# Three regroupings in a perceiver layer, and one of four channel pairs convolved by diagonal matrices

## The chip, the cores and the metric

The kernel runs on one core of a Trainium2 chip. Its engines work side by side and meet only at semaphores: PE multiplies matrices into PSUM, DVE (VectorE), ACT (ScalarE) and POOL (GpSimd) work element by element, SP issues the transfers. The metric is the device time of one execution in microseconds; lower is better.

## What is computed

The reference is a layer of three parts with residual sums, on x of 16 x 128 x 512 and a context of 16 x 2048 x 512, all in fp32. The change touches the first and the second.

```python
x = x + xattn(layernorm(x), ctx, wq, bq, wk, bk, wv, bv, wo, bo)     # 16 heads
x = x + mamba_and_mlp(layernorm(x), ...)
x = x + ffn(layernorm(x), ...)

def _mamba(Z, ...):
    xz = jnp.einsum('bld,ed->ble', Z, in_proj_w)
    x, z = jnp.split(xz, 2, axis=-1)
    x = jax.nn.silu(_causal_dw_conv(x, conv_w, conv_b))              # 4 taps, per channel
    x_dbl = jnp.einsum('bld,ed->ble', x, x_proj_w)
    dt, Bm, Cm = jnp.split(x_dbl, [DTR, DTR + DS], axis=-1)
    dt = jax.nn.softplus(jnp.einsum('blr,dr->bld', dt, dt_proj_w) + dt_proj_b)
    # h = exp(dt * A) * h + dt * B * x;  y = sum over 16 states of h * C, step by step
    y = y + x * D
    y = y * jax.nn.silu(z)
    return jnp.einsum('bld,ed->ble', y, out_proj_w)
```

## The kernel before

It has three stages with a barrier between them: `cross_attention`, `mamba`, `feed_forward`.

**The query stretch** opens `cross_attention`. Four blocks of x (4 batches each, 1 MB) go through `normalise` on DVE (statistics, then four TENSOR_SCALARs, L339), with the reciprocal root on POOL between the two (L236, L238), sixteen transposes (L459) and 96 matmuls in two halves (L477) on PE. DVE also splits the weights in this stretch. POOL adds bo to each block after its normalisation (L242, waits for `xn_ready`), SP stores it to `x_scratch`. Two buffers in `probs` hold x, so block 2 is loaded after block 0 is stored. Then the loop over 16 batches begins, with key projections (L498) and loads of the context into `c_raw`.

**mamba** takes eight steps of two batches (256 tokens). Inner channels are eight chunks of 128, in four pairs. The recurrence runs as 32 units in a step: unit m is channel pair m // 8 and two of the 16 states. In each unit ACT fills `decay` in PSUM (a copy and four exponentials, L1073, L1077; two slots), POOL makes `drive` = dt_u * B (L939; four slots, free again when PE has summed), DVE scans (L1212) and multiplies by C (L1223), PE adds both states into `b_y` by two matmuls with the identity (L1356, semaphore `summed`). At units 8, 16, 24 and the next step's unit 0 DVE multiplies the finished pair by its gate (L1177): it waits there for PE's last b_y, and PE then starts the next pair with two matmuls for D (L1352).

Between these the next step's preparation is laid out by numbers at the top of the function, each the unit behind which a piece is issued on its engine: head projections, layernorm, transposes, x projections (units 9, 10, 11, 13), z projections (L1271; eight halves), taps on ACT and three shifted multiply-adds per chunk on DVE (L1149; units 12, 13, 14, 16), silu of u (L1008, unit 18), the x_dbl product (L1297, unit 19), dt projections (21, 23), and then softplus: ACT takes absolute value, exponential (units 25 and 27) and logarithm (L1045), POOL the rounding error of 1 + e: (e + 1) - 1 in one TENSOR_SCALAR (L906), and e minus that (L908), behind units 28 and 31; then the two sums of dt (L912, L914) and dt_u (L920). Every order is fixed in the program; an engine stops at the first wait that is not met. Steps 1 to 6 run in a loop of three turns with two steps each.

## Time and profile before

| | us |
|---|---|
| median of 3 runs | 4165.88 (4165.74 to 4169.53) |
| profiled execution | 4164.47 |
| its span, first to last instruction | 4162.3 |

| stage | us | PE busy | DVE | ACT | POOL |
|---|---|---|---|---|---|
| query stretch, 0 to 77 | 77 | 56.7 | 49.4 | 19.9 | 31.0 |
| attention, to 2424 | 2347 | 2311.5 | 1558.4 | 854.8 | 290.1 |
| mamba, first step's preparation, to 2497 | 73 | 45.9 | 23.0 | 23.7 | 6.1 |
| mamba, 256 units, to 3609 | 1112 | 944.3 | 998.1 | 691.9 | 821.0 |
| feed-forward, to 4162 | 553 | 512.5 | 244.3 | 117.7 | 57.9 |

The busy times come from the view that sums each engine over stretches of time. In a timeline a row gives start, length, engine, line, operation, output and inputs, and in brackets how long the engine stood idle before and who released it. Consecutive instructions overlap a little, so distances between starts say more than lengths. The first key projection (L498) starts at 77.15. A step of mamba takes 141.3 us: the TENSOR_SCALAR at L906 recurs at that distance, from 2610.4 to 3458.2 seven times.

### The profile page before, as it was taken

The page shows a single profiled execution, that of the slowest core. Times are in us where ns is not written, and L with a number is a line of the kernel's source. Part 1 is how long each engine was busy: PE and PEld are TensorE (multiplying, and loading weights), DVE is VectorE, ACT ScalarE, POOL GpSimd, SP SyncE. Part 2 cuts the span into 40 slices and gives each one's busy share as a digit, 9 for nine tenths or more (in the row PEclk, how much of TensorE's full clock was granted, in tenths as well). Part 3 has the DMA queues.
Part 4 walks back from the last instruction along what each step waited for, and adds up shares of the span by engine and source line. Part 5 has one row for each costly group of instructions (what it writes and reads, how often), then busy time and mean ns, then how long its engine had stood idle before and what let it go on. Part 6 is the DMA issues. An engine that isn't in the chain of part 4 may idle for free. (4 is left out here: it accounts for less than half of the span.)

```text
span 4162.3 us, 85144 instructions
## 1 busy us (share of the span) xinstructions
PE 3870.9 (93%) x34816; PEld 2798.7 (67%) x34816; DVE 2873.2 (69%) x3019; ACT 1707.9 (41%) x3434; POOL 1206.1 (29%) x563
## 2 busy tenths in 40 slices
PE   7999999999999999999999968888888887599998
PEld 6777877777787777777777755445444443288876
DVE  6667667766766776676667649889988988764433
ACT  2324423433442443344244346666566656322221
POOL 3111010111011011101100106876787678420000
PEclk9999999999999999999999989999999999899999
DMA  5010010011001001100100030211011111120000
GB/s 190 32 36 28 35 44 27 25 44 37 28 32 47 27 25 44 37 28 32 46 28 22 24 128 26 61 51 46 26 61 51 36 35 46 58 87 26 30 20 16
DMA packets 94278, 179.23 MB, mean 43 GB/s; under 512 B 7889, under 2 KB 12369, under 8 KB 93938
## 3 DMA queue, kind: packets, MB, share of 16 engines
q1 hardware_dynamic: 93938, 174.08, 12.8%
q8 instruction: 289, 4.73, 0.5%
q14 instruction: 51, 0.42, 0.0%
HBM read 148.63 MB, written 25.43 MB: 42 GB/s over the span
## 5 line engine op out<-in xcount | busy, mean ns | idle before, releaser
L230 POOL TENSOR_TENSOR c_lo<-c_raw,c_hi 128x2048 fp32r<-128x2048 f32 x64 | 294.9, 4608 | 1987.0 <-DVE c_hi L323 1987.0
L939 POOL TENSOR_TENSOR b_drive<-b_dt_u,b_bc 128x1024 f32<-128x1024 f32 x256 | 600.7, 2357 | 284.9 <-PE b_y L1356 248.7
L1356 PE MATMUL b_y<-b_drive,b_ident 128*128 128x512 f32 x1024 | 512.2, 627 | 146.7 <-DVE b_drive L1223 146.7
L412 DVE TENSOR_TENSOR prob_sums<-prob_sums,probs 128x1024 f32<-128x1024 f32 x480 | 566.7, 1222 | 114.0 <-ACT probs L295 114.0
L1212 DVE TENSOR_TENSOR_SCAN b_decay<-b_decay,b_drive 128x1024 f32<-128x1024 f32 x256 | 585.9, 2289 | 80.3 <-POOL b_drive L939 62.1
L384 DVE TENSOR_REDUCE max_parts<-scores 128x2 f32<-128x1024 f32 x512 | 601.8, 1218 | 40.3 <-PE scores L546 40.3
L295 ACT ACTIVATE probs<-scores 128x512 f32<-128x512 f32 x1024 | 529.0, 603 | 213.9 <-PE scores L577 213.9
L376 DVE SCALAR_TENSOR_TENSOR k_lo<-scores,bk_sb,k_hi 128x512 fp32r<-128x512 f32 x256 | 192.3, 751 | 562.0 <-ACT k_hi L280 561.9
L1356 PEld LDWEIGHTS b_y<-b_drive,b_ident 128*128 128x128 f32 x1024 | 188.9, 196 | 395.9 <-DVE b_drive L1223 236.4
L1077 ACT ACTIVATE b_decay<-b_dt,b_a 128x254 f32<-128x254 f32 x1024 | 425.0, 461 | 0.4
L280 ACT ACTIVATE k_hi<-scores,bk_sb 128x512 fp32r<-128x512 f32 x256 | 176.4, 689 | 603.1 <-PE scores L498 603.1
L288 ACT COPY v_sb<-scores 128x512 f32<-128x512 f32 x240 | 141.1, 588 | 668.4 <-PE scores L498 668.4
L1223 DVE TENSOR_TENSOR b_drive<-b_decay,b_bc 128x1024 f32<-128x1024 f32 x256 | 313.0, 1223 | 7.8
L577 PE MATMUL scores<-q_hi,k_lo 32*128 32x128 f32 x4096 | 305.3, 270 | 0.0
L577 PE MATMUL scores<-q_lo,k_hi 32*128 32x128 f32 x4096 | 305.1, 270 | 0.0
L577 PE MATMUL scores<-q_hi,k_hi 32*128 32x128 f32 x4096 | 291.8, 256 | 0.0
L498 PE MATMUL scores<-c_hi,wk_hi 128*128 128x512 f32 x1024 | 287.4, 402 | 0.0
L498 PE MATMUL scores<-wv_hi,c_hi 128*128 128x512 f32 x960 | 281.2, 415 | 0.0
L591 PE MATMUL o_acc<-probs,v_sb 128*32 128x128 f32 x8192 | 276.7, 276 | 1.2 <-ACT probs L295 1.2
L498 PE MATMUL scores<-c_hi,wk_lo 128*128 128x512 f32 x1024 | 274.8, 390 | 0.0
L498 PE MATMUL scores<-c_lo,wk_hi 128*128 128x512 f32 x1024 | 273.7, 389 | 0.0
L498 PE MATMUL scores<-wv_lo,c_hi 128*128 128x512 f32 x960 | 258.7, 391 | 0.0
(219 smaller groups left out, 6304.9 us busy)
## 6 DMA issues: line engine op xcount, KB each, us to landing
c_raw<-in_ctx SPq DMA_DIRECT2D x64, 1024.0 KB, 5.1
b_bc<-bc_scratch SPq DMA_DIRECT2D x128, 256.0 KB, 4.2
probs<-in_x SPq DMA_DIRECT2D x4, 1024.0 KB, 5.6
x_scratch<-probs SPq DMA_DIRECT2D x4, 1024.0 KB, 6.0
q_scratch<-v_sb SPq DMA_DIRECT2D x4, 1024.0 KB, 4.4
q_raw<-q_scratch SPq DMA_DIRECT2D x16, 256.0 KB, 2.9
attn_scratch<-attn_out_sb SPq DMA_DIRECT2D x16, 256.0 KB, 2.0
b_attn<-attn_scratch SPq DMA_DIRECT2D x8, 512.0 KB, 4.1
```

The lines of the kernel that those rows point to most:

```text
L230: pool.tensor_tensor(c_lo[:, slot], c_raw[:], c_hi[:, slot].bitcast(F32), ALU.subtract).then_inc(c_lo_ready, 1)
L295: act.activation(probs[:, (2 * t + j // 2) % 4, j % 2, :], score_bank(t, j), ACT.Exp, scale=scale).then_inc(exp_done, 1)
L384: dve.tensor_reduce(max_parts[:, g, 2 * pair:2 * pair + 2, s], max_banks[:, 2 * pair:2 * pair + 2, :], AX.X, ALU.max).then_inc(max_taken, 1)
L412: dve.tensor_tensor(part, part, probs[:, u % 4], ALU.add).then_inc(summed, 1)
L498: ins = pe.matmul(out, lhs, rhs, start=(m == 0), stop=(m == len(steps) - 1))
L577: ins = pe.matmul(banks[j][:, g * queries:(g + 1) * queries], k_part[head_rows(j), g, ts], q_part[head_rows(j), g, :], start=False, stop=last,
L591: ins = pe.matmul(o_acc[head_rows(j), g * queries:(g + 1) * queries], v_sb[:, t, h * hd:(h + 1) * hd], probs[:, (2 * t + j // 2) % 4, j % ...
L939: pool.tensor_tensor(drive[:, m % 4], dt_u[:, 2 * p:2 * p + 2, :].unsqueeze(1).to_broadcast([P, SG, 2, T]), bc[:, g, 0].unsqueeze(2).to_br ...
L1077: ins = act.activation(slot[:, q:q + group, 1:], by_batch(dt[:, par, c, :])[:, :, 1:], ACT.Exp, scale=a_neg[:, c, g * SG + s:g * SG + s + 1])
L1212: dve.tensor_tensor_scan(decay[:, m % 2], decay[:, m % 2], drive[:, m % 4].rearrange("p n c t -> p (n c t)"), 0.0, ALU.mult, ALU.add).then ...
L1223: dve.tensor_tensor(drive[:, m % 4], decay[:, m % 2].rearrange("p (n c t) -> p n c t", c=2, t=T), bc[:, g, 1].unsqueeze(2).to_broadcast([P ...
L1356: ins = pe.matmul(y_ps[:], ident[:], drive[:, m % 4, s].rearrange("p c t -> p (c t)"), start=False, stop=(g == groups - 1 and s == SG - 1) ...
```

## The change

- Query stretch: the x blocks lie in `probs`, `c_raw`, `probs`, `probs`, so three loads need no store before them. On POOL the additions of bo come later than before, each behind a following rstd or behind the first low part of the context. The first context load comes after the second x store, and the last two x stores after the last query store.
- mamba: the first half of the rounding error, (e + 1) - 1, is made by DVE behind units 25 and 27 (`round_sum`); POOL keeps the subtraction.
- mamba: silu of the gate, before at unit 30 of the step ahead (in step 0 at unit 3), is at unit 4 of its own step.
- mamba: channel pair 3 (chunks 6 and 7) is convolved on PE. POOL makes eight diagonal matrices of the taps once. ACT copies the projection to `u` (behind unit 16), PE multiplies four shifted views by the diagonals into the same PSUM bank (behind unit 15), ACT's silu reads that bank and adds the bias. Three z projection halves move one unit back (15, 16, 17 to 16, 17, 18).

```diff
@@ cross_attention
-        x_sb = [probs[:, 2 * par:2 * par + 2].rearrange("p n j d -> p (n j) d") for par in range(2)]
+        x_even, x_odd = (probs[:, 2 * n:2 * n + 2].rearrange("p n j d -> p (n j) d") for n in range(2))
+        x_sb = [x_even, c_raw[:], x_odd, x_even]
@@ sync
+            load_x(2)
+            store_x(0)
+            sp.wait_ge(x_stored, 16)
+            load_x(3)
+            store_queries(0)
+            sp.wait_ge(q_stored, 16)
+            sp.dma_start(q_raw[:], q_dram[0]).then_inc(q_loaded, 16)
+            store_x(1)
+            sp.wait_ge(x_stored, 2 * 16)
             load(0, 0)
-            for i in range(q_steps):
-                sp.wait_ge(bo_added, i + 1)
-                sp.dma_start(x_out_v[i], x_sb[i % 2]).then_inc(x_stored, 16)
-                if i + 2 < q_steps:
-                    sp.wait_ge(x_stored, (i + 1) * 16)
-                    load_x(i + 2)
+            for i in range(1, q_steps):
                 store_queries(i)
-                if i == 0:
-                    sp.wait_ge(q_stored, 16)
-                    sp.dma_start(q_raw[:], q_dram[0]).then_inc(q_loaded, 16)
+            store_x(2)
+            store_x(3)
             sp.wait_ge(q_stored, q_steps * 16)
             sp.wait_ge(x_stored, q_steps * 16)
@@ gpsimd
+            make_rstd(0)
+            make_rstd(1)
+            pool.wait_ge(bo_loaded, 16)
+            add_bo(0)
+            make_rstd(2)
+            add_bo(1)
+            make_rstd(3)
+            low_part(0, 0)
+            add_bo(2)
+            add_bo(3)
@@ mamba
-    PE_IN_Z, PE_OUT = (14, 15, 16, 17, 20, 22, 24, 25), (27, 29, 31)
+    PE_IN_Z, PE_OUT = (14, 16, 17, 18, 20, 22, 24, 25), (27, 29, 31)
...
+    DVE_M = (25, 27)
+    PE_CONV = 15
+    taken = pairs - 1
@@ gpsimd
             def rounding_error(j, h):
 
-                pool.wait_ge(exp_ready, j * 2 + h + 1)
-                pool.tensor_tensor(pool_wait_taker[:], zeros[:, 0:1], zeros[:, 0:1], ALU.add)
-                pool.tensor_scalar(e_round[h], e_neg[h], 1.0, -1.0, ALU.add, ALU.add).then_inc(rounded, 1)
                 pool.wait_ge(rounded, j * 2 + h + 1)
                 pool.tensor_tensor(e_neg[h], e_neg[h], e_round[h], ALU.subtract).then_inc(low_ready, 1)
...
+                pool.wait_ge(x_half_loaded, X_HALF_LOADED)
+                pool.tensor_tensor(tap_diag[:], ident[:].unsqueeze(1).unsqueeze(1).to_broadcast([P, 2, taps, P]),
+                                   conv_w_sb[:, 2 * taken:, :].unsqueeze(3).to_broadcast([P, 2, taps, P]),
+                                   ALU.mult).then_inc(tap_diag_ready, 1)
@@ scalar
+            def copy_last(j, par):
+                act.wait_ge(x_product, (j + 1) * pairs)
+                act.copy(u[:, par, 2 * taken:, :],
+                         work[:, x_bank(taken), :].rearrange("p (c t) -> p c t", t=T)).then_inc(x_copied, 1)
+
             def silu_u(j, par):
                 for h in range(2):
-                    act.wait_ge(x_taken, j * pairs + (h + 1) * (pairs // 2))
-                    hc = slice(h * half, (h + 1) * half)
-                    ins = act.activation(u[:, par, hc, :], u[:, par, hc, :], ACT.Silu)
+                    act.wait_ge(x_taken, j * taken + (2, taken)[h])
+                    hc = slice(h * half, min((h + 1) * half, 2 * taken))
+                    act.activation(u[:, par, hc, :], u[:, par, hc, :], ACT.Silu)
+                act.wait_ge(convolved, j + 1)
+                for cc in range(2):
+                    c = 2 * taken + cc
+                    ins = act.activation(u[:, par, c, :], work[:, x_bank(taken), cc * T:(cc + 1) * T], ACT.Silu,
+                                         bias=conv_b_sb[:, c:c + 1])
                 ins.then_inc(u_ready, 1)
@@ vector, body
+                    if m in DVE_M:
+                        round_sum(j, DVE_M.index(m))
@@ tensor
+            def convolve_last(j, par):
+                pe.wait_ge(x_copied, j + 1)
+                for cc in range(2):
+                    out = by_batch(work[:, x_bank(taken), cc * T:(cc + 1) * T])
+                    x_in = by_batch(u[:, par, 2 * taken + cc, :])
+                    for shift in range(taps):
+                        ins = pe.matmul(out[:, :, shift:], tap_diag[:, cc, taps - 1 - shift], x_in[:, :, 0:seq - shift],
+                                        start=(shift == 0), stop=(shift == taps - 1), skip_group_check=True)
+                ins.then_inc(convolved, 1)
```

On PE the place is units 14 to 16 of the first step; b_work holds projections, b_y the sum over states. Before:

```order
L1356 MATMUL b_y<-b_drive,b_ident 128x512 x2
L1271 MATMUL b_work<-b_xn_t,b_w_in 128x256 x4
L1356 MATMUL b_y<-b_drive,b_ident 128x512 x2
L1271 MATMUL b_work<-b_xn_t,b_w_in 128x256 x4
L1352 MATMUL b_y<-b_u,b_d_diag 128x256 x2
L1356 MATMUL b_y<-b_drive,b_ident 128x512 x2
```

After:

```order
L1412 MATMUL b_y<-b_drive,b_ident 128x512 x2
L1315 MATMUL b_work<-b_xn_t,b_w_in 128x256 x4
L1412 MATMUL b_y<-b_drive,b_ident 128x512 x2
L1334 MATMUL b_work<-b_u,b_tap_diag 128x256
L1334 MATMUL b_work<-b_u,b_tap_diag 128x2x127
L1334 MATMUL b_work<-b_u,b_tap_diag 128x2x126
L1334 MATMUL b_work<-b_u,b_tap_diag 128x2x125
L1334 MATMUL b_work<-b_u,b_tap_diag 128x256
L1334 MATMUL b_work<-b_u,b_tap_diag 128x2x127
L1334 MATMUL b_work<-b_u,b_tap_diag 128x2x126
L1334 MATMUL b_work<-b_u,b_tap_diag 128x2x125
L1408 MATMUL b_y<-b_u,b_d_diag 128x256 x2
```

A z projection half that stood behind unit 15 is replaced by eight matmuls with the tap diagonals.

On POOL the place is unit 28 of the first step, where x and attn are the buffers of e and of its rounded sum. Before:

```order
L939 TENSOR_TENSOR b_drive<-b_dt_u,b_bc 128x1024 x21
L905 TENSOR_TENSOR b_pool_wait_taker<-b_zeros 128x1
L906 TENSOR_SCALAR b_attn<-b_x 128x1024
L908 TENSOR_TENSOR b_x<-b_x,b_attn 128x1024
L939 TENSOR_TENSOR b_drive<-b_dt_u,b_bc 128x1024 x2
L912 TENSOR_TENSOR b_dt<-b_dt,b_attn 128x1024
```

After:

```order
L966 TENSOR_TENSOR b_drive<-b_dt_u,b_bc 128x1024 x21
L931 TENSOR_TENSOR b_x<-b_x,b_attn 128x1024
L966 TENSOR_TENSOR b_drive<-b_dt_u,b_bc 128x1024 x2
L935 TENSOR_TENSOR b_dt<-b_dt,b_attn 128x1024
L937 TENSOR_TENSOR b_dt<-b_dt,b_x 128x1024
```

Two of the three instructions between the drives are gone.

On DVE the place is units 24 and 25 of the first step. Before:

```order
L1177 TENSOR_TENSOR b_gate<-b_y,b_gate 128x512
L1223 TENSOR_TENSOR b_drive<-b_decay,b_bc 128x1024
L1212 SCALAR_TENSOR_TENSOR b_decay<-b_decay,b_drive 128x1024
L1223 TENSOR_TENSOR b_drive<-b_decay,b_bc 128x1024
L1212 SCALAR_TENSOR_TENSOR b_decay<-b_decay,b_drive 128x1024
```

After:

```order
L1219 TENSOR_TENSOR b_gate<-b_y,b_gate 128x512
L1265 TENSOR_TENSOR b_drive<-b_decay,b_bc 128x1024
L1254 SCALAR_TENSOR_TENSOR b_decay<-b_decay,b_drive 128x1024
L1265 TENSOR_TENSOR b_drive<-b_decay,b_bc 128x1024
L1196 TENSOR_SCALAR b_attn<-b_x 128x1024
L1254 SCALAR_TENSOR_TENSOR b_decay<-b_decay,b_drive 128x1024
```

The TENSOR_SCALAR stands behind the multiply of unit 25.

On POOL in the query stretch, from the first rstd on. Before:

```order
L236 TENSOR_TENSOR q_rstd<-q_moments,q_eps 128x4
L238 TENSOR_TENSOR q_rstd<-q_rstd,q_minus_half 128x4
L242 TENSOR_TENSOR probs<-probs,attn_out_sb 128x2048
L236 TENSOR_TENSOR q_rstd<-q_moments,q_eps 128x4
L238 TENSOR_TENSOR q_rstd<-q_rstd,q_minus_half 128x4
L242 TENSOR_TENSOR probs<-probs,attn_out_sb 128x2048
```

After:

```order
L244 TENSOR_TENSOR q_rstd<-q_moments,q_eps 128x4
L246 TENSOR_TENSOR q_rstd<-q_rstd,q_minus_half 128x4
L244 TENSOR_TENSOR q_rstd<-q_moments,q_eps 128x4
L246 TENSOR_TENSOR q_rstd<-q_rstd,q_minus_half 128x4
L250 TENSOR_TENSOR probs<-probs,attn_out_sb 128x2048
L244 TENSOR_TENSOR q_rstd<-q_moments,q_eps 128x4
```

The addition of bo to block 0 stood between the rstd of blocks 0 and 1 and now follows that of block 1.

## Rows read from the trace of the kernel before

**Rows 1.** Timeline of DVE: start and length in us, instruction, count, [idle before <- releaser].

```profile
2886.31 0.69 DVE L1177 TENSOR_TENSOR b_gate<-b_y,b_gate 128x512 f32<-128x512 f32 x1 [2.25 <-PE b_y L1356]
...
2888.05 2.29 DVE L1212 TENSOR_TENSOR_SCAN b_decay<-b_decay,b_drive 128x1024 f32<-128x1024 f32 x1
...
2891.51 2.29 DVE L1212 TENSOR_TENSOR_SCAN b_decay<-b_decay,b_drive 128x1024 f32<-128x1024 f32 x1
...
2903.75 2.30 DVE L1212 TENSOR_TENSOR_SCAN b_decay<-b_decay,b_drive 128x1024 f32<-128x1024 f32 x1 [1.76 <-ACT b_decay L1077]
...
2912.74 2.30 DVE L1212 TENSOR_TENSOR_SCAN b_decay<-b_decay,b_drive 128x1024 f32<-128x1024 f32 x1 [1.98 <-POOL b_drive L939]
...
2921.23 2.30 DVE L1212 TENSOR_TENSOR_SCAN b_decay<-b_decay,b_drive 128x1024 f32<-128x1024 f32 x1 [4.93 <-POOL b_drive L939]
...
2934.13 2.30 DVE L1212 TENSOR_TENSOR_SCAN b_decay<-b_decay,b_drive 128x1024 f32<-128x1024 f32 x1 [1.97 <-POOL b_drive L939]
...
2994.64 0.69 DVE L1177 TENSOR_TENSOR b_gate<-b_y,b_gate 128x512 f32<-128x512 f32 x1 [0.56 <-PE b_y L1356]
...
2996.39 2.67 DVE L1149 SCALAR_TENSOR_TENSOR b_u<-b_work,b_conv_w,b_u 128x254 f32<-128x254 f32 x6
...
3027.75 0.69 DVE L1177 TENSOR_TENSOR b_gate<-b_y,b_gate 128x512 f32<-128x512 f32 x1 [2.25 <-PE b_y L1356]
```

**Rows 2.** Timeline of POOL across units 28 to 31, same columns.

```profile
2891.05 2.36 POOL L939 TENSOR_TENSOR b_drive<-b_dt_u,b_bc 128x1024 f32<-128x1024 f32 x1 [2.34 <-PE b_y L1356]
...
2893.51 3.65 POOL L906 TENSOR_SCALAR b_attn<-b_x 128x1024 f32<-128x1024 f32 x1
...
2897.25 2.35 POOL L908 TENSOR_TENSOR b_x<-b_x,b_attn 128x1024 f32<-128x1024 f32 x1
...
2909.06 1.27 POOL L920 TENSOR_TENSOR b_dt_u<-b_dt,b_u 128x512 f32<-128x512 f32 x1
```

**Rows 3.** Timeline of DVE in the first step's preparation.

```profile
2485.04 0.69 DVE L1158 TENSOR_SCALAR b_attn<-b_x 128x1024 f32<-128x1024 f32 x1 [11.93 <-ACT b_x L1040]
```

**Rows 4.** Timeline of POOL and DVE in the query stretch.

```profile
23.60 1.02 POOL L238 TENSOR_TENSOR q_rstd<-q_rstd,q_minus_half 128x4 f32<-128x4 f32 x1
...
24.66 1.92 DVE L339 TENSOR_SCALAR prob_sums<-probs,q_moments,q_rstd 128x512 f32<-128x512 f32 x4 [1.42 <-POOL q_rstd L238]
...
56.42 1.22 DVE L323 CAST c_hi<-c_raw 128x2048 fp32r<-128x2048 f32 x1
...
56.58 5.50 POOL L242 TENSOR_TENSOR probs<-probs,attn_out_sb 128x2048 f32<-128x2048 f32 x1 [2.03 <-DVE prob_sums L339]
...
60.50 1.85 DVE L369 CAST q_hi<-q_raw 128x512 fp32r<-128x512 f32 x1
...
62.03 4.80 POOL L230 TENSOR_TENSOR c_lo<-c_raw,c_hi 128x2048 fp32r<-128x2048 f32 x1
```

**Rows 5.** Timeline of ACT from unit 28 to the next step's unit 0.

```profile
2896.87 1.28 ACT L1045 ACT_TABLE_LOAD   x1
...
2899.63 1.06 ACT L1045 ACTIVATE b_attn<-b_attn 128x1024 f32<-128x1024 f32 x1 [1.47 <-POOL b_x L908]
...
2902.05 1.66 ACT L1077 ACTIVATE b_decay<-b_dt,b_a 128x254 f32<-128x254 f32 x4
...
2907.20 1.91 ACT L1018 ACTIVATE b_gate<-b_gate 128x2048 f32<-128x2048 f32 x1
...
2916.13 0.17 ACT L1073 COPY b_decay<-b_zeros 128x8 f32<-128x8 f32 x1 [3.99 <-issue]
```

**Rows 6.** Timeline of PE: first step's x_dbl product, then units 19 to 21.

```profile
2474.21 3.64 PE L1297 MATMUL b_work<-b_u,b_w_x 128*64 128x256 f32 x16 [1.55 <-ACT b_u L1008]
...
3009.49 1.98 PE L1356 MATMUL b_y<-b_drive,b_ident 128*128 128x512 f32 x4 [1.48 <-DVE b_drive L1223]
...
3016.83 1.89 PE L1271 MATMUL b_work<-b_xn_t,b_w_in 128*128 128x256 f32 x8
...
3018.55 1.88 PE L1356 MATMUL b_y<-b_drive,b_ident 128*128 128x512 f32 x4
```

67 lines of the change are left out of this document (40 added, 27 removed).

## The prediction

> **What bounds the kernel now.** I read the busy time by stage first, then the idle times of the engine that is busiest there, then the timelines of the engines it waits for. The three stages follow one another: attention to about 2424 us, mamba to about 3620, feed-forward to the end. In mamba VectorE (DVE) is the busiest, at nine tenths in the table of stages above. One unit of its work is a scan and a multiply, 3.46 us (2888.05 to 2891.51) [rows 1], and a step has 32 of them. The bracket at a row's end is the idle time before it, and who ended it [rows 1]: per step DVE waits 2.25 us for PE's b_y at unit 24, 1.76 for ACT's decay at unit 29, 1.98, 4.93 and 1.97 for POOL's drive at units 31, 0 and 3. These five recur in all seven step boundaries to within 0.05 us (the last four add up to 10.64 us per step). POOL is late because from unit 28 on it has the rounding error (3.65 + 2.35 us, and again at unit 31) and the sums of dt to do between drives of 2.35 us each [rows 2]. So mamba is a DVE chain with holes that POOL makes; attention is bound by PE and not touched; in the stretch before it (to 77 us) PE waits for DVE.
>
> **Round sums moved from POOL to DVE.** POOL loses 3.65 us twice per step [rows 2]. DVE gains two TENSOR_SCALARs of 128x1024, behind the multiplies of units 25 and 27. The same form cost DVE 0.69 us where POOL stood idle [rows 3]. Beside a running POOL no row shows it; the nearest is the cast at 60.50: 1.85 us for 512 columns, where 2048 columns took 1.22, and it ended just after POOL's 56.58 + 5.50 = 62.08 [rows 4]. So I take it that the sum waits until the POOL instruction that is running has ended: 0.65 to 3.05 us each. The phase says how long. Count from the gate multiply at unit 24 (2886.31 = 0). POOL's drive for unit 28 started at 2891.05, released by PE's b_y of unit 24, and this release doesn't move: 4.74 to 7.10. The first sum is due at 5.2, starts at 7.1, and the next scan at 7.75 instead of 5.2: 2.55 us. POOL subtracts 7.8 to 10.15, makes two drives (the second is released by b_y of unit 26, at 13.15) until 15.5; the second sum is due at 14.75 and costs 0.75 + 0.65 = 1.4 us.
>
> What goes: ACT's logarithm needs POOL's subtraction, now at 10.15. Its fill of unit 28 starts with multiply 26 (11.3) and ends at 13.1; table load 1.28 and logarithm 1.06 [rows 5] to 15.5; table load and fill of unit 29 to 18.6, and scan 29 is due at 16.2 + 3.46 = 19.65. The 1.76 go. POOL: dt sums 16.2 to 20.9, dt_u 1.27 to 22.1, drive 31 to 24.5 (due 26.6: the 1.98 go), subtraction to 26.8, drive 0 to 29.15 (due 30.05: the 4.93 go), dt_u, drives 1 and 2 to 35.1, two dt sums to 39.8, drive 3 to 42.15, due 41.0: 1.2 of the 1.97 stay. Sum: 10.64 - 2.55 - 1.4 - 1.2 = 5.5 us per step.
>
> **Silu of the gate, from unit 30 of the step before to unit 4.** Two table loads and 1.9 us [rows 5] leave the place where ACT is pressed. At unit 4 ACT has fill 4 done at about 42.9 on the same count, silu to 46.1, table and fill 5 to 49.1; DVE comes for unit 5 at 52.1. Nothing is late there, and at the old place the wait went already: 0.
> ACT's loop has two steps per turn, and behind the branch back ACT stood 3.99 us with nothing to wait for [rows 5]. Today this is hidden under the 4.93. Then: fill 31 ends at 25.0, + 4.0, fill of unit 0 to 30.85, due 30.05. 0.8 us on two branches: 1.6 us.
>
> **The convolution of pair 3 on PE.** DVE loses six instructions at unit 16, 2.58 us from row to row (2996.39 to 2998.97, of which the first stands in [rows 1]). PE gains eight matmuls of 256 columns in fp32; four of that form take 1.72 us, from 3016.83 to 3018.55 [rows 6], so 3.45 us, with their weight loads in it. Is there room? The interval between the gate multiplies of units 16 and 24 is 33.1 us (2994.64 to 3027.75) [rows 1], and it ends with a wait for PE: from 3009.49 on [rows 6] PE works without a gap, 18.3 us. In the new order PE has from the end of b_y 15: 3.45 + 0.86 (two matmuls for D) + 3 x 1.72 (b_y 16 to 18) + 3 x 1.72 (z projections, one of them moved here) = 14.6, and then the same 18.3: 32.9 us. The old idle gaps of PE at units 17 and 19 are where it fits. b_y 15 ends some 0.2 before the multiply, so the interval becomes 32.7: **0.4 us of the 2.58** is kept, the rest turns into a longer wait for b_y at unit 24 (about 4.4 less what ACT takes, below). ACT's part is one copy for two scaled taps, and a silu in four pieces that now reads PE's result at 3.5; with it the fill of unit 19 comes 1.85 late. That lies under PE's lateness: 0. In the first step there is no cover: the z projection stands ahead of the x_dbl product, which waited 1.55 us for u [rows 6]; it comes 4.15 - 1.55 = 2.6 us later. POOL's new diagonal tiles are made while it idles: 0.
>
> **The query stretch.** The third x block no longer waits for a buffer, but little waited for it. The order on POOL matters: adding bo to block 0 now stands right behind the second rstd. Before it came after DVE's normalisation, by a wait. POOL's pow ended at 24.62 and DVE started at 24.66 [rows 4]; two POOL instructions in a row start without a gap (56.58 + 5.50 and 62.03), so POOL would be first. If the four TENSOR_SCALARs of the normalisation are held like the cast, they come 4.6 us late, and again at block 2; PE waits for them. The stretch from turn 1 to turn 2 becomes 14.2 - 0.75 + 4.6, from 2 to 3 about as long as now, less 1; the first projection of keys, at 77.15 in the table above, starts 5.1 later. The next context load waits for two x stores that are now queued behind the last query store: 0.7. Together **5.8 us lost**, bounds -1.4 and 10.
>
> **The sum.** 7 x (5.5 + 0.4) = 41.3; less 1.6, 2.6 and 5.8: 31.3 us. The profiled execution took 4164.5 (span 4162.3); it becomes 4133.2. The runs' median is 1.4 above it: **4134.5 us**.
>
> Two rules of the Trainium skill bear on this. SBUF — State Buffer, "Who interferes with whom", says that a DVE instruction in a two-port mode and a GpSimd instruction exclude each other for the whole length of the one that started first; the row at 60.50 agrees, and without the rule the two sums would cost 1.3 instead of 3.95 us and the time be 18 us lower. Runtime: NRT & Kernel Launch, "Instruction fetch mechanics", says that a taken branch to a target outside the two held blocks of instructions stalls; ACT's 3.99 us agrees, and for DVE it would give the third rival.
>
> **Rivals.** *A, the query stretch loses nothing* (DVE gets in first, or this form isn't held): 4134.5 - 5.8 = 4129. For it: 0.54 us for 512 columns is no clean double rate. Chance 0.22.
> *B, the round sums are not held:* 3.95 becomes 1.3 per step, 7 x 2.65 = 18.6 us: 4116. Chance 0.12.
> *C, DVE too stalls behind its branch back*, which is hidden today under the wait of 4.93: about 3.5 us on two turns, 4141. Against: its loop body has some 300 instructions in the order of the program, ACT's some 500. Chance 0.06.
> *D, PE is worse off than counted:* a matmul whose columns lie in two runs of 127 to 125 costs twice what the plain one of the rows does: 3.4 us per step, all at unit 24: 4158. Chance 0.09.
> *E, slower:* a held DVE instruction is not let in between two POOL instructions that follow at once. The second sum, due at 14.75, then waits through dt sums, dt_u and drive 31, to 23.8: 8.3 us per step, 58 us: 4193. It decides from a POOL queue without a gap at 15.5. Against: the cast at 60.50 got in between two such instructions, and the second took 0.2 longer. Chance 0.05.
> *F, the gain goes to a wait not seen:* 4166. Chance 0.06.
> The forecast itself: 0.40.
>
> **Numbers.** 0.2% (8.3 us) is about what a measurement tells from no change. Faster: forecast, A, B, C and half of D, 0.85 with a rest of F: 0.87. Same: half of D and most of F: 0.07. Slower: E and a rest: 0.06. The range leaves out E, F and the far half of D: 4112 (B with its slack) to 4152 (C or a cheap D).
>
> **What would show it.** Right: DVE's waits for POOL at units 31 and 0 gone, about 1 us at unit 3; TENSOR_SCALARs of 2.5 and 1.4 us on DVE; wait for b_y at unit 24 grown to 2.5 to 4.5 us; step 135.4 instead of 141.3 us; normalisations of blocks 1 and 2 with a TENSOR_SCALAR of some 5 us; first key projection at 82. Wrong: sums of 0.7 us, step of 133 or of over 139 us, a b_y wait over 6 us, first key projection before 78.

## The result, and the profile after

The changed kernel takes 4137.44 us (median of 4 runs, 4134.2 to 4138.92) against 4165.81 us before; the ratio is 0.9929, 95% interval 0.9912 to 0.9946. The prediction said 4134.5 us. The profiled execution has a span of 4136.4 us, 25.9 less than before.

Where the two executions part, from the timelines (us from the start of each):

| point | before | after | difference |
|---|---|---|---|
| first key projection | 77.15 | 82.56 | +5.4 |
| first reciprocal behind attention's last batch | 2420.34 | 2426.62 | +6.3 |
| scan of unit 0, step 0 | 2497.55 | 2506.46 | +8.9 |
| gate multiply at unit 24, step 0 | 2603.16 | 2610.89 | +7.7 |
| last gate multiply of mamba | 3604.54 | 3577.48 | -27.1 |
| end of span | 4162.3 | 4136.4 | -25.9 |

The stretches before the first scan lose 8.9 us, the eight steps win 36.0, 34.8 of them from the first step's unit 24 on; 1.2 are lost again in feed-forward. Busy times by engine, from the top of the page:

```profile
PE 3890.2 (94%) x34944; PEld 2826.2 (68%) x34944; DVE 2885.8 (70%) x2985; ACT 1706.0 (41%) x3442; POOL 1157.0 (28%) x536
```

POOL is 49.1 us less busy (1206.1 before), DVE 12.6 more: it has fourteen more sums (two had been its own in the first step's preparation), and fewer multiply-adds.

**A step's boundary.** Timeline of DVE from the gate multiply at unit 24 on, the rows that answer to [rows 1]; then POOL beside it:

```profile
2881.53 0.69 DVE L1219 TENSOR_TENSOR b_gate<-b_y,b_gate 128x512 f32<-128x512 f32 x1 [2.84 <-PE b_y L1412]
...
2885.59 1.23 DVE L1265 TENSOR_TENSOR b_drive<-b_decay,b_bc 128x1024 f32<-128x1024 f32 x1
2886.73 2.44 DVE L1196 TENSOR_SCALAR b_attn<-b_x 128x1024 f32<-128x1024 f32 x1
2889.09 2.28 DVE L1254 TENSOR_TENSOR_SCAN b_decay<-b_decay,b_drive 128x1024 f32<-128x1024 f32 x1
...
2896.02 1.64 DVE L1196 TENSOR_SCALAR b_spare<-b_mix 128x1024 f32<-128x1024 f32 x1
2897.58 2.28 DVE L1254 TENSOR_TENSOR_SCAN b_decay<-b_decay,b_drive 128x1024 f32<-128x1024 f32 x1
...
2914.17 2.30 DVE L1254 TENSOR_TENSOR_SCAN b_decay<-b_decay,b_drive 128x1024 f32<-128x1024 f32 x1 [2.66 <-POOL b_drive L966]
...
2950.73 0.69 DVE L1219 TENSOR_TENSOR b_gate<-b_y,b_gate 128x512 f32<-128x512 f32 x1 [1.67 <-PE b_y L1412]
```

```profile
2889.25 2.35 POOL L931 TENSOR_TENSOR b_x<-b_x,b_attn 128x1024 f32<-128x1024 f32 x1 [0.63 <-DVE b_attn L1196]
...
2897.07 2.80 POOL L935 TENSOR_TENSOR b_dt<-b_dt,b_attn 128x1024 f32<-128x1024 f32 x1
...
2908.23 2.35 POOL L966 TENSOR_TENSOR b_drive<-b_dt_u,b_bc 128x1024 f32<-128x1024 f32 x1
```

The waits of 1.76, 1.98 and 4.93 us at units 29, 31 and 0 are gone. In their place stand two sums of 2.44 and 1.64 us; from start to start they push the next scan back by 2.36 (2886.73 to 2889.09) and 1.56 us. At unit 0 a wait of 2.66 us stands in this step and one of 2.68 at 3189.70, the two places where the loop branches back, and in none of the others. In the other five steps the wait for POOL's drive at unit 3 is 1.25 us, against 1.97 before:

```profile
2652.97 2.30 DVE L1254 TENSOR_TENSOR_SCAN b_decay<-b_decay,b_drive 128x1024 f32<-128x1024 f32 x1 [1.25 <-POOL b_drive L966]
```

The sum of dt at 2897.07 took 2.80 us where the other sum of dt, at 2899.95, took 2.36: it started while DVE's second sum ran (2896.02 to 2897.66). So POOL is held by DVE as well.

**PE's clock.** DVE's wait for b_y at unit 8 (2950.73) is 1.67 us; it is 0 in five of the seven steps. Timeline of PE ahead of it, and the table of windows, whose fields are the window, its length, busy time and count of PE, its weight loads, DVE, ACT and POOL, then the granted clock, the DMA share and GB/s:

```profile
2938.37 1.98 PE L1412 MATMUL b_y<-b_drive,b_ident 128*128 128x512 f32 x4 [0.98 <-DVE b_drive L1265]
2943.45 2.72 PE L1412 MATMUL b_y<-b_drive,b_ident 128*128 128x512 f32 x4 [3.10 <-DVE b_drive L1265]
2946.91 3.78 PE L1412 MATMUL b_y<-b_drive,b_ident 128*128 128x512 f32 x4 [0.74 <-DVE b_drive L1265]
```

```profile
2940.00:2944.00 4.00, 0.90 (x3) 0.31 (x3) 3.96 (x3) 2.05 (x8) 3.77 (x6) 1.00 0.00 0
2944.00:2948.00 4.00, 3.26 (x6) 0.94 (x5) 3.96 (x3) 3.75 (x10) 3.92 (x4) 0.57 0.10 39
2948.00:2952.00 4.00, 4.00 (x13) 2.34 (x12) 2.33 (x3) 0.65 (x2) 4.00 (x3) 0.58 0.24 94
2952.00:2956.00 4.00, 2.60 (x8) 1.06 (x7) 3.97 (x4) 2.75 (x7) 3.29 (x2) 1.00 0.00 0
```

Four matmuls that take 1.98 us take 3.78: behind the idle 3.10 us the granted clock is 0.57 and 0.58 for two windows of 4 us, that is the lower of its two levels, 1.2 instead of 2.4 GHz, for most of them. The trace of before has such falls too. One less the granted clock, summed over windows of 2 us from 2520 to the last gate multiply, is the clock lost in the steps: 25.6 us there (15 falls of 1.7 us each) and 18.8 here (11 falls). But there DVE's six waits at units 8 and 16 add up to 3.2 us, and the six here to 6.8.

**The query stretch.** Timelines of DVE and POOL at block 1, to be read against [rows 4], and of PE at its end:

```profile
24.02 6.12 DVE L360 TENSOR_SCALAR prob_sums<-c_raw,q_moments,q_rstd 128x512 f32<-128x512 f32 x4 [1.41 <-POOL q_rstd L246]
```

```profile
22.97 1.01 POOL L246 TENSOR_TENSOR q_rstd<-q_rstd,q_minus_half 128x4 f32<-128x4 f32 x1
23.95 4.54 POOL L250 TENSOR_TENSOR probs<-probs,attn_out_sb 128x2048 f32<-128x2048 f32 x1
```

```profile
82.56 1.07 PE L519 MATMUL scores<-c_hi,wk_hi 128*128 128x512 f32 x4
```

POOL starts the addition of bo 0.07 us ahead of the four TENSOR_SCALARs, and these take 6.12 instead of 1.92 us: the addition ends at 28.49, they end at 30.14. Block 2 repeats it (42.63, 6.13 us).

### The profile page after: what moved, and what is told of

Read it like the earlier page. It is cut to its first block and busy times, and to the rows that moved or that the text cites. A ratio compares the mean times of both kernels' runs of the same rounds, so it can differ in the third digit from the quotient of the medians.

```text
span 4136.4 us, 85345 instructions
## 1 busy us (share of the span) xinstructions
PE 3890.2 (94%) x34944; PEld 2826.2 (68%) x34944; DVE 2885.8 (70%) x2985; ACT 1706.0 (41%) x3442; POOL 1157.0 (28%) x536
## 5 line engine op out<-in xcount | busy, mean ns | idle before, releaser
L1412 PE MATMUL b_y<-b_drive,b_ident 128*128 128x512 f32 x1024 | 502.9, 619 | 116.0 <-DVE b_drive L1265 116.0
```

The source lines that it names most:

```text
L1412: ins = pe.matmul(y_ps[:], ident[:], drive[:, m % 4, s].rearrange("p c t -> p (c t)"), start=False, stop=(g == groups - 1 and s == SG - 1) ...
```

## The experiments

All kernels are the changed one with the edit that is shown; the times are medians of 4 to 11 runs, the ratios are to the kernel before in the same session, which took 4164.6 to 4167.9 us.

| kernel | us | ratio to before | interval |
|---|---|---|---|
| query_old | 4131.5 | 0.9921 | 0.9907 to 0.9934 |
| sum_stt | 4151.4 | 0.9970 | 0.9958 to 0.9982 |
| conv_dve | 4132.5 | 0.9925 | 0.9911 to 0.9938 |
| sums_pool | 4172.7 | 1.0016 | 1.0007 to 1.0025 |
| gate30 | 4140.3 | 0.9946 | 0.9932 to 0.9960 |
| dve_unroll | 4132.8 | 0.9921 | 0.9907 to 0.9935 |
| sums_early | 4115.9 | 0.9883 | 0.9867 to 0.9899 |
| best1 | 4106.2 | 0.9862 | 0.9846 to 0.9877 |
| warm | 4128.8 | 0.9912 | 0.9899 to 0.9926 |
| best2 | 4097.9 | 0.9835 | 0.9821 to 0.9848 |
| best3 | 4094.6 | 0.9829 | 0.9815 to 0.9842 |
| best4 | 4092.0 | 0.9820 | 0.9807 to 0.9833 |

The four runs of the changed kernel lie between 4134.2 and 4138.9 us. Those of conv_dve (4131.3 to 4136.6) and of gate30 (4136.9 to 4145.1) overlap with them, and so do those of best2 and best3 with each other (4094.9 to 4098.5, 4092.2 to 4096.2): what is said of these small differences rests on the rows.

### The order on POOL in the query stretch (query_old)

```diff
             make_rstd(0)
-            make_rstd(1)
             pool.wait_ge(bo_loaded, 16)
             add_bo(0)
-            make_rstd(2)
+            make_rstd(1)
             add_bo(1)
+            make_rstd(2)
+            add_bo(2)
             make_rstd(3)
             low_part(0, 0)
-            add_bo(2)
             add_bo(3)
```

> The changed kernel, with bo added on POOL directly behind each block's own normalisation again (reciprocal root 0, bo 0, reciprocal root 1, bo 1, reciprocal root 2, bo 2, reciprocal root 3, first low part, bo 3); buffers, loads and stores stay as changed. The changed kernel took 4137.4 us. Theory (two TENSOR_SCALAR groups were held 4.2 us each by the addition of bo that started 0.07 us ahead of them): the groups of blocks 1 and 2 take 1.9 us instead of 6.1, the two casts of wk and wv are held 0.7 us each instead, and the first key projection comes at about 76 instead of 82.56: 6 to 7 us less, 4131. Rival (the stretch is late for another reason, such as the stores and the loads behind them on SP): first key projection at 81 or later, 4137.

Measured: 4131.5 us. Timelines of DVE, POOL and PE:

```profile
24.61 1.92 DVE L360 TENSOR_SCALAR prob_sums<-c_raw,q_moments,q_rstd 128x512 f32<-128x512 f32 x4 [1.42 <-POOL q_rstd L246]
...
30.77 1.52 DVE L337 CAST wk_hi<-v_sb 128x2048 fp32r<-128x2048 f32 x1
```

```profile
26.61 4.60 POOL L250 TENSOR_TENSOR c_raw<-c_raw,attn_out_sb 128x2048 f32<-128x2048 f32 x1 [2.03 <-DVE prob_sums L360]
```

```profile
73.95 1.07 PE L519 MATMUL scores<-c_hi,wk_hi 128*128 128x512 f32 x4
```

The group of four is back at 1.92 us, a cast pays 0.3 (and its like at 44.52 0.8), and the key projections start 8.6 us earlier than in the changed kernel (some 6.5 were expected), 3.2 earlier than before. So the new buffers and loads are worth 3.2 us, and the two moved additions cost 8.6. The medians moved by 5.9 and the spans by 8.6: the attention stretch behind, to the reciprocal of the first table, is itself 2342.2 to 2345.3 us long in the profiles of the fourteen kernels, though nothing in it differs.

### Where the gain of the boundary comes from (sums_pool, gate30)

```diff
+                pool.wait_ge(exp_ready, j * 2 + h + 1)
+                pool.tensor_tensor(pool_wait_taker[:], zeros[:, 0:1], zeros[:, 0:1], ALU.add)
+                pool.tensor_scalar(e_round[h], e_neg[h], 1.0, -1.0, ALU.add, ALU.add).then_inc(rounded, 1)
                 pool.wait_ge(rounded, j * 2 + h + 1)
...
-                    if m in DVE_M:
-                        round_sum(j, DVE_M.index(m))
```

> The changed kernel, with the round sum back on POOL (3.65 us twice per step), silu of the gate staying at unit 4. Theory (the sums are the whole gain of the step boundaries): waits for POOL of about 2.0, 4.9 and 2.0 us at units 31, 0 and 3 are back and the sums of 2.4 and 1.6 us on DVE are gone; 5.75 us more per step, less 2.7 on the two turns where DVE's wait of 2.66 at unit 0 is hidden again: 35 more, 4172. Rival (moving silu of the gate away from unit 30 has removed part of the waits): units 31 and 0 wait less than 5 us together, below 4160.

Measured: 4172.7 us. Timeline of DVE across one boundary:

```profile
2771.60 2.30 DVE L1257 TENSOR_TENSOR_SCAN b_decay<-b_decay,b_drive 128x1024 f32<-128x1024 f32 x1 [1.76 <-ACT b_decay L1118]
...
2780.57 2.30 DVE L1257 TENSOR_TENSOR_SCAN b_decay<-b_decay,b_drive 128x1024 f32<-128x1024 f32 x1 [1.95 <-POOL b_drive L969]
...
2789.06 2.30 DVE L1257 TENSOR_TENSOR_SCAN b_decay<-b_decay,b_drive 128x1024 f32<-128x1024 f32 x1 [4.93 <-POOL b_drive L969]
...
2801.96 2.30 DVE L1257 TENSOR_TENSOR_SCAN b_decay<-b_decay,b_drive 128x1024 f32<-128x1024 f32 x1 [1.97 <-POOL b_drive L969]
```

All four waits of [rows 1] are back to within 0.03 us, although silu of the gate stayed at unit 4. Without the moved sums nothing is gained at the boundary; the new place of the silu alone brings nothing. Units 24 to 0 take 37.10 us in all seven steps here, and 32.11 in the changed kernel where it does not branch.

```diff
-    ACT_Z, ACT_DBC, ACT_ABS, ACT_EXP, ACT_LOG0, ACT_GATE = (19, 20, 25, 29), 22, (24, 26), (25, 27), 28, 4
+    ACT_Z, ACT_DBC, ACT_ABS, ACT_EXP, ACT_LOG0, ACT_GATE = (19, 20, 25, 29), 22, (24, 26), (25, 27), 28, 30
...
-                        silu_gate(i, par)
+                        silu_gate(j, 1 - par)
```

> The changed kernel, with silu of the gate at unit 30 of the step before again. Theory (it has slack at either place): at unit 30 the silu and its two table loads make ACT's fill of unit 31 about 1.2 us late on DVE's scan of unit 31, but POOL's chain from unit 27 to unit 3 is not moved, so the wait of 1.25 at unit 3 becomes as much shorter: the period of a step stays 134.5 us (without lateness of PE), the time within 3 us of 4137. Rival (the place at unit 4 is part of the gain): 1.2 us or more per step is lost, 4146 or more.

Measured: 4140.3 us. Timeline of DVE:

```profile
2774.70 2.30 DVE L1256 TENSOR_TENSOR_SCAN b_decay<-b_decay,b_drive 128x1024 f32<-128x1024 f32 x1 [1.16 <-ACT b_decay L1115]
...
2789.70 2.30 DVE L1256 TENSOR_TENSOR_SCAN b_decay<-b_decay,b_drive 128x1024 f32<-128x1024 f32 x1 [0.60 <-POOL b_drive L966]
```

ACT is 1.16 us late at unit 31, and the wait at unit 3 shrinks from 1.25 to 0.60. Units 24 to 8 take 66.65 instead of 66.05 us, 0.6 us per step; the medians differ by 2.9. The move was called free at both places; it is worth a little, once the waits behind it have become short.

### What holds the sum (sum_stt, sums_early)

```diff
-                dve.tensor_scalar(e_round[h], e_neg[h], 1.0, -1.0, ALU.add, ALU.add).then_inc(rounded, 1)
+                dve.scalar_tensor_tensor(e_round[h], e_neg[h], 1.0, minus_one[:].to_broadcast([P, group * width]),
+                                         ALU.add, ALU.add).then_inc(rounded, 1)
```

> The changed kernel, with the round sum (e + 1) - 1 on DVE in the steps' units written as a SCALAR_TENSOR_TENSOR, (e + 1) + (a column of -1, broadcast), instead of a TENSOR_SCALAR. Theory (only the short form, 0.69 us for 1024 columns, is held by a running POOL instruction; a form that takes 1.2 us for 1024 columns, as the multiply does, runs beside POOL): both sums take 1.2 us instead of 2.44 and 1.64, DVE gains 1.64 us per step; POOL's chain from unit 27 to unit 3 starts 1.2 earlier and its sum of dt is no longer held 0.45, so the wait at unit 3 stays near 1.25: 1.6 to 1.7 us per step, 11.5 in seven: 4126. Rival (any DVE instruction issued at that point waits for POOL, whatever its form): 1.2 + 1.8 and 1.2 + 0.9 us: 7 us more, 4144. Second rival (the wait at unit 3 and the stall at unit 0 take it back): step time unchanged, 4137.

Measured: 4151.4 us; the theory fell. Timelines of DVE and POOL:

```profile
2617.01 2.98 DVE L1198 SCALAR_TENSOR_TENSOR b_attn<-b_x,b_minus_one 128x1024 f32<-128x1024 f32 x1
...
2625.69 1.22 DVE L1269 TENSOR_TENSOR b_drive<-b_decay,b_bc 128x1024 f32<-128x1024 f32 x1
2626.84 2.18 DVE L1198 SCALAR_TENSOR_TENSOR b_spare<-b_mix,b_minus_one 128x1024 f32<-128x1024 f32 x1
...
2902.86 1.22 DVE L1198 SCALAR_TENSOR_TENSOR b_spare<-b_mix,b_minus_one 128x1024 f32<-128x1024 f32 x1
```

```profile
2616.55 2.35 POOL L968 TENSOR_TENSOR b_drive<-b_dt_u,b_bc 128x1024 f32<-128x1024 f32 x1 [2.35 <-PE b_y L1416]
...
2625.58 2.36 POOL L968 TENSOR_TENSOR b_drive<-b_dt_u,b_bc 128x1024 f32<-128x1024 f32 x1 [0.85 <-PE b_y L1416]
2627.89 3.34 POOL L937 TENSOR_TENSOR b_dt<-b_dt,b_attn 128x1024 f32<-128x1024 f32 x1
...
2903.25 3.03 POOL L968 TENSOR_TENSOR b_drive<-b_dt_u,b_bc 128x1024 f32<-128x1024 f32 x1 [2.51 <-PE b_y L1416]
```

The long form is held as well: it ends 1.09 us after POOL's drive (2616.55 + 2.35 = 2618.90), about its own length. A multiply of the same size and pace is not: the one at 2625.69 starts 0.11 us behind POOL's drive at 2625.58 and takes its 1.22. They differ in where the inputs lie (the multiply's first is decay, in PSUM, the sum's two are in SBUF) and in the operation; no run parts the two.

The second sum shows the rest within one execution. Its length over the seven steps is 2.18, 3.32, 1.22, 2.17, 3.24, 2.82 and 2.18 us, by where POOL's drive has got to. At 2902.86 the sum starts 0.39 us ahead of the drive, takes 1.22, and it is the drive that is held: 3.03 instead of 2.35. In the four steps that differ the drive was released later, behind PE at the lower clock, in that one so late that DVE came first. From start to start the fourteen sums cost 9.4 us more than those of the changed kernel; the rival's 4144 is 7 short of the time. The rest was not followed up; PE's lost clock, summed as above, is 32.4 us in this execution against 18.8.

The Trainium skill, SBUF — State Buffer, "Who interferes with whom", states the case: a DVE instruction with both inputs in SBUF contends with a GpSimd instruction that reads SBUF. I had drawn on that section only for the two-port modes; by its other sentence the rival was the one to expect, and these rows agree.

```diff
                         end_pair(i - 1, 1 - par, pairs - 1)
+                    if not last and m in DVE_M:
+                        round_sum(j, DVE_M.index(m))
                     dve.wait_ge(scanned, i * units + m + 1)
...
-                    if m in DVE_M:
-                        round_sum(j, DVE_M.index(m))
```

> The changed kernel, with each round sum between the scan and the multiply of units 25 and 27 instead of behind the multiply, 1.14 us earlier. Nothing else is changed; the sum stays a TENSOR_SCALAR. Theory (what counts is whether a POOL instruction is under way when it is due): counted from the gate multiply of unit 24, POOL is idle until 4.74 and the sum starts at 4.03 and takes 0.7 instead of 2.44; the second is due at 11.6 and waits 0.2 for POOL to end: 0.9 instead of 1.64; DVE gains 2.4 us per step, POOL's chain starts 0.8 earlier and is not held 0.45, so the wait at unit 3 grows from 1.25 to about 2.4 and 1.25 us per step are kept: 8.8 in seven: 4128.5. Rival (the length of the sum does not depend on POOL's phase): sums of 2.4 and 1.6 us again, 4137.

Measured: 4115.9 us, 21.5 less than the changed kernel where 8.8 were expected. (The profiled execution is the slowest of the four, 4119.1.) Timelines of DVE and POOL; the gate multiply of this step starts at 2613.50:

```profile
2617.44 0.68 DVE L1196 TENSOR_SCALAR b_attn<-b_x 128x1024 f32<-128x1024 f32 x1
...
2624.82 0.97 DVE L1196 TENSOR_SCALAR b_spare<-b_mix 128x1024 f32<-128x1024 f32 x1
...
2787.04 2.30 DVE L1254 TENSOR_TENSOR_SCAN b_decay<-b_decay,b_drive 128x1024 f32<-128x1024 f32 x1 [1.99 <-POOL b_drive L966]
```

```profile
2613.55 2.35 POOL L966 TENSOR_TENSOR b_drive<-b_dt_u,b_bc 128x1024 f32<-128x1024 f32 x1 [1.08 <-PE b_y L1412]
2618.25 2.36 POOL L966 TENSOR_TENSOR b_drive<-b_dt_u,b_bc 128x1024 f32<-128x1024 f32 x1 [2.34 <-PE b_y L1412]
```

0.68 us in POOL's idle time, at 3.94 from the gate multiply, and 0.97 us at 11.3: moved by one multiply's length, the two sums are 1.65 us long together instead of 4.08. The wait at unit 3 grows to 1.99, as it must while POOL's chain is the later one (0.87 to 0.89 in two steps, where DVE had waited 1.0 us for PE at unit 0), and the period without a disturbance is 133.05 instead of 134.46 us: 1.41 per step, 9.9 in seven. That is what the edit does. In the profiled executions 19.4 us lie between the two kernels. Of the rest, about 8 us are PE at the lower clock, of which DVE feels here one wait at units 8 and 16 instead of six; why, no run shows. 2.5 us are DVE's stall at the branches, which now hides under the longer wait at unit 3.

### DVE's own branch (dve_unroll)

In the changed kernel the profile names POOL's drive as the releaser of the scan at 2914.17. But the drive had started at 2908.23 and was done at 2910.6, and ACT's decay was done at 2911.7:

```profile
2909.93 0.17 ACT L1111 COPY b_decay<-b_zeros 128x8 f32<-128x8 f32 x1 [3.55 <-issue]
2910.04 1.66 ACT L1115 ACTIVATE b_decay<-b_dt,b_a 128x254 f32<-128x254 f32 x4
```

```diff
-            run_steps(dve, front, body, finish)
+            run_steps(dve, front, body, finish, True)
```

With `True`, the six middle steps are written out one after another for DVE instead of looped over.

> The changed kernel, with DVE's six middle steps of the second stage written out instead of three turns of a loop; the other engines keep their loops. In the changed kernel DVE stood 2.66 and 2.68 us before the scan of unit 0 at both branches back, with its drive made 3.6 us earlier and its decay filled 2.5 us earlier. Theory (that is DVE's own branch, which the 4.93 hid before): both waits fall to 0.2 (ACT's decay, late by its own branch), the wait of about 1.25 for POOL at unit 3 comes back in these two steps: 2 x 1.2 = 2.4 less, 4135. Rival (a drive or a decay is late there): the waits of 2.7 stay, 4137.

Measured: 4132.8 us. Timeline of DVE at the first of the two places:

```profile
2915.91 2.30 DVE L1259 TENSOR_TENSOR_SCAN b_decay<-b_decay,b_drive 128x1024 f32<-128x1024 f32 x1 [0.75 <-ACT b_decay L1120]
...
2927.24 2.30 DVE L1259 TENSOR_TENSOR_SCAN b_decay<-b_decay,b_drive 128x1024 f32<-128x1024 f32 x1 [0.40 <-POOL b_drive L971]
```

The stall of 2.66 is gone, ACT's lateness of 0.75 shows, and the wait at unit 3 is back at 0.40. So the stall was DVE's own branch, hidden under the 4.93 of before: rival C, which I had given 0.06. Units 24 to 8 of these two steps take 65.9 and 67.2 us (with a wait of 1.20 for PE in the latter) against 69.2 (with one of 1.67) and 67.5 in the changed kernel, and 65.9 in the steps without a branch: the two branches no longer cost anything. The medians differ by 4.6, more than the 2.8 that the branches had cost in the changed kernel's profile.

The rule that the prediction named for it, from the Trainium skill's Runtime: NRT & Kernel Launch, "Instruction fetch mechanics", agrees with a stall at DVE's shorter loop; that the target lay outside what DVE held, no run here shows.

### The convolution on PE (conv_dve)

```diff
-    PE_CONV = 15
-    taken = pairs - 1
+    taken = pairs
-    DVE_SUM, DVE_X1, DVE_CONV = 4, (3, 5), (12, 13, 14)
+    DVE_SUM, DVE_X1, DVE_CONV = 4, (3, 5), (12, 13, 14, 16)
```

with the projections and taps at the units of before.

> The changed kernel, with channel pair 3 convolved on DVE again (taps on ACT behind unit 17, six shifted multiply-adds behind unit 16, z projections behind 14, 15, 16, 17). Theory (PE has no room, so that of DVE's 2.58 us per step only 0.55 was kept, and the first step paid 2.6): units 16 to 24 take 33.1 instead of 32.5 us, the wait for b_y at unit 24 is 2.25 instead of 2.64, the first step starts 2.6 earlier: 7 x 0.55 - 2.6 = 1.3 more, 4139, within 3 us of the changed kernel either way. Rival (the convolution on PE brought most of its 2.58 us): 18 - 2.6 = 15 more, 4153.

Measured: 4132.5 us, 4.9 less than the changed kernel. Timeline of DVE, the scan of unit 0 in the first step:

```profile
2502.19 2.30 DVE L1240 TENSOR_TENSOR_SCAN b_decay<-b_decay,b_drive 128x1024 f32<-128x1024 f32 x1 [2.55 <-ACT b_decay L1103]
```

Units 16 to 24 take 33.08 to 33.10 us with a wait of 2.25 for b_y, against 32.52 with 2.64. So PE's convolution keeps 0.56 us per step, 3.9 in seven, and it costs 2.75 us in the first step (from the reciprocal of the first table to the first scan: 77.09 against 79.84). By these two the kernel should be 1.2 slower; it is 4.9 faster in the medians and 7.2 in the spans. What differs otherwise is PE's lower clock, which costs the steps of this execution 3.9 us, by waits at unit 16, and those of the changed one 9.8 in all (the count is shown below); 1.5 us lie in the attention stretch and 1.0 in feed-forward. Whether the convolution on PE makes the clock fall at worse places, this pair does not tell: among the kernels without zero matmuls that have it, 1 to 5 of seven steps have a wait for b_y at unit 16, and 2 to 4 among those that have not. So the two counted terms stand. Between their sum and the result the clock fills 5.9 us in these two executions, and that the convolution is its cause is not shown.

### Holding the clock up (warm)

```diff
+    PE_WARM = {5: 3, 6: 1, 14: 2}
...
+                    for _ in range(PE_WARM.get(m, 0)):
+                        pe.matmul(y_ps[:], ident[:], zeros[:, 0:1].to_broadcast([P, 512]),
+                                  start=False, stop=False, skip_group_check=True)
```

> The changed kernel, with six more matmuls per step on PE that add zeros into b_y (identity as weights, a broadcast zero as the moving side): three behind unit 5, one behind unit 6, two behind unit 14, where PE stood 3.10, 0.7 and 2.33 us idle. They do no useful work. Theory (the granted clock fell to its lower level behind these idle stretches, a b_y pair then took 3.6 instead of 1.9 us, and DVE waited 0.4 to 1.7 us at units 8 and 16 for it): in the steps no wait for b_y over 0.3 us at units 8 and 16, units 16 to 24 take 32.5 us in all of them: the 6.6 us of waits at units 8 and 16 and 2.4 us of longer units 16 to 24 are gone: 9 less, 4128. Rival (the clock falls whatever PE does there, or the added matmuls come in the way of b_y): waits at units 8 and 16 stay at 6 us or more over the steps, 4137 or more.

Measured: 4128.8 us (4128.4 to 4129.7). Timeline of PE at units 5 and 6, and the windows:

```profile
2938.41 2.75 PE L1436 MATMUL b_y<-b_zeros,b_ident 128*128 128x512 f32 x6
2941.67 1.99 PE L1413 MATMUL b_y<-b_drive,b_ident 128*128 128x512 f32 x4 [0.52 <-DVE b_drive L1266]
```

```profile
2940.00:2944.00 4.00, 3.48 (x9) 1.25 (x7) 3.93 (x4) 2.35 (x6) 4.00 (x2) 1.00 0.00 0
2944.00:2948.00 4.00, 3.38 (x15) 1.70 (x13) 4.00 (x4) 2.62 (x7) 3.92 (x5) 1.00 0.35 133
```

From the first step's unit 4 to the last unit the granted clock does not fall once, no wait for b_y at units 8 and 16 is left, and the four periods without a branch last 134.45 to 134.49 us. In the changed kernel the same four range from 134.46 to 136.18, and the two with a branch are 139.34 and 137.61 against 136.10 and 136.21 here. Six matmuls of zeros per step are worth 8.6 us in the medians. The same idle stretches of PE recur in every step of the changed kernel, and the clock fell behind some of them only (not behind one of 2.33 us at 2710.77, say).

### All together (best1 to best4)

best1 has the edits of query_old, conv_dve, sums_early, DVE and ACT written out, and POOL's dt_u of pair 1 behind unit 3 instead of 0.

```diff
-    POOL_DT_U1, POOL_DT_H1, POOL_DT_U2, POOL_DT_U3, POOL_RSTD, POOL_OUT = 0, 2, 4, 5, 7, 9
+    POOL_DT_U1, POOL_DT_H1, POOL_DT_U2, POOL_DT_U3, POOL_RSTD, POOL_OUT = 3, 2, 4, 5, 7, 9
```

> What the theories together ask for: bo added on POOL behind each block's normalisation (-6), pair 3 convolved on DVE (-5), round sums between scan and multiply of units 25 and 27, POOL's dt_u of pair 1 behind unit 3 instead of unit 0, which makes its drive of unit 3 ready 1.3 us earlier (the two together -3.6 per step, -25), and DVE and ACT with their six middle steps written out (-5). Theory: 4137.4 - 41 = 4096, steps of 131.5 us, no wait for POOL over 0.3 us at units 31, 0 and 3. Rival (POOL's chain from unit 27 on bounds the boundary whatever moves in it): waits for POOL at units 2 to 5 of over 2 us per step, 4112 or more.

Measured: 4106.2 us, 10 more than expected. The waits at unit 3 kept 0.76 us in the five steps where DVE had not waited for PE at unit 0, and DVE waited 0.6 to 1.7 us for b_y eight times in the steps, at units 8, 16 and 0. Hence the next two: best2 adds the zero matmuls and the split of the two dt sums over units 2 and 3, best3 is best2 with the convolution back on PE.

```diff
-    POOL_DT_U1, POOL_DT_H1, POOL_DT_U2, POOL_DT_U3, POOL_RSTD, POOL_OUT = 3, 2, 4, 5, 7, 9
+    POOL_DT_U1, POOL_DT_H1, POOL_DT_U2, POOL_DT_U3, POOL_RSTD, POOL_OUT = 5, (2, 3), 8, 10, 7, 9
```

> The combination of before (bo behind each normalisation, pair 3 convolved on DVE, round sums between scan and multiply, DVE and ACT written out), with the six zero matmuls, POOL's two dt sums of the second half behind units 2 and 3 instead of both behind 2, and dt_u of pairs 1, 2 and 3 behind units 5, 8 and 10. The combination without these two took 4106.2 us; it waited 0.76 for POOL at unit 3 in every step and 6.8 us in all for b_y at units 8 and 16. Theory: both go: 5.3 + 6.8 = 12 less, 4094; steps of 132.1 - 0.8 = 131.3 us. Rival (the waits at units 8 and 16 come back elsewhere): 4100 or more, steps over 132.

> As the kernel of this call that is convolved on DVE, but with pair 3 convolved on PE as in the change. Theory (PE's convolution keeps 0.55 us per step and costs 2.75 in the first step's preparation, and with the clock held up nothing else): within 1.5 us of the other, 4093; units 16 to 24 take 32.5 instead of 33.1 us, the first scan comes 2.75 later. Rival (PE's convolution leaves DVE more exposed to PE being late, and is worth -5 us as when it was undone alone): 4099.

Measured: 4097.9 and 4094.6 us. No wait for POOL at unit 3 is left, the undisturbed periods are 131.24 and 130.68 us. With the clock held up at units 5 to 15, the convolution on PE keeps 0.56 us per step and costs 2.3 in the first step's preparation, as beside conv_dve, and it is the better one by 3.3 us in the medians, where these two terms give 1.6. In both the clock still fell where PE stands 1.92 us idle ahead of unit 27's b_y, and DVE waited 1.0 us at unit 0 in four steps and two steps.

best4 starts from best3:

```diff
-    PE_IN_Z, PE_OUT = (14, 16, 17, 18, 20, 22, 24, 25), (27, 29, 31)
-    PE_WARM = {5: 3, 6: 1, 14: 2}
+    PE_IN_Z, PE_OUT = (14, 14, 16, 17, 20, 22, 24, 25), (27, 29, 31)
+    PE_WARM = {5: 3, 6: 1, 26: 2}
```

> The best kernel so far (pair 3 on PE, bo behind each normalisation, early round sums, split dt sums, zero matmuls, DVE and ACT written out; 4094.6 us), with the second z projection half behind unit 14 instead of unit 16 and the following ones one place earlier (14, 14, 16, 17, 20, 22, 24, 25), so that it takes the place of the two zero matmuls there; two zero matmuls behind unit 26. Theory (DVE's wait of 2.63 us for b_y at unit 24 is the sum of PE's work since the b_y of unit 15, as the prediction counted it): one half less is 1.72 us, the wait falls to 0.9 us and units 16 to 24 take 30.8 instead of 32.5: 12 us less in seven steps, and 2 us less for the two waits of 1.00 at unit 0: 4081. Rival (PE waits there for ACT's copies and the silu of u, not for its own work): units 16 to 24 stay at 32 us or more, 4092.

Measured: 4092.0 us, ratio 0.9820 to before. Units 16 to 24 take 32.14 us: 0.38 less, not 1.72. Timelines of PE and DVE:

```profile
2845.79 1.98 PE L1423 MATMUL b_y<-b_drive,b_ident 128*128 128x512 f32 x4 [1.08 <-DVE b_drive L1278]
```

```profile
2842.18 2.30 DVE L1265 TENSOR_TENSOR_SCAN b_decay<-b_decay,b_drive 128x1024 f32<-128x1024 f32 x1 [1.55 <-ACT b_decay L1126]
...
2864.05 0.69 DVE L1230 TENSOR_TENSOR b_gate<-b_y,b_gate 128x512 f32<-128x512 f32 x1 [2.26 <-PE b_y L1423]
```

PE now stands idle 1.08 us before the b_y of unit 19, since DVE's scan of unit 19 waits 1.55 us for ACT's decay. From there PE works without a gap for 18.3 us to the b_y that ends pair 2, just as in the trace of before. The half that was taken away lay ahead of that point, and ACT had become the later one there; the rival was right. The waits at unit 0 are gone, with two zero matmuls behind unit 26; the median is 2.6 us lower.

## Why the prediction was right, point by point

The time was 2.9 us above the forecast of 4134.5, and the profiled execution 5.3 above the 4133.2 that the sum gave for it (4138.5; 25.9 us of span were won instead of 31.3). That it came so near is in part luck: the steps won more than was forecast, and a term of 6 us was missing. Sum against measurement, in us, from the profiles:

| term | predicted | measured |
|---|---|---|
| first sum, cost on DVE | 2.55 | 2.36 |
| second sum | 1.4 | 1.56 |
| waits left at units 29, 31, 0, 3 | 0, 0, 0, 1.2 | 0, 0, 0, 1.25 |
| gain of a boundary, per step | 5.5 | 5.74 |
| convolution on PE, per step | 0.4 | 0.56 |
| seven steps | 41.3 | 44.1 |
| branches back | -1.6 | -2.8 |
| PE at the lower clock | 0 | -6.0 |
| first step's preparation | -2.6 | -2.6 |
| query stretch | -5.8 | -5.4 to -6.3 |
| feed-forward | 0 | -1.2 |

(The gain of a boundary: units 24 to 0 went from 37.13 to 32.11, and the wait at unit 3 from 1.97 to 1.25. The branches: units 24 to 0 of the two steps took 34.85 and 34.89 us instead of 32.11, and units 0 to 8 gave 1.34 of it back each time, 32.60 instead of 33.94. In warm, where DVE stood 2.89 and 3.00 us, the two cost 3.4. The clock: the six periods between unit 24 and unit 24 add up to 819.4 us, six undisturbed ones of 134.46 to 806.8; less the 2.8 that leaves 9.8. The same count of before, 847.8 less six of 140.76, leaves 3.2, and 0.6 in the last step (69.12 us from unit 24 to 8, against 68.51 in sums_pool). Feed-forward took 558.9 against 557.8 us; it ranges from 557.4 to 559.3 in the fourteen profiles, and the cause was not followed up. With the -6.3 the measured column adds up to 25.2 of the 25.9 us; the rest is, to 0.1, what the first step won besides its convolution.)

- **The bound.** DVE's chain with holes made by POOL was right: sums_pool brings the holes back, and the gain with them.
- **The hold of the sums.** Right in its mechanism and nearly in its size, by counting POOL's phase from the gate multiply. sums_early shows it from the other side: the same instruction 1.14 us earlier costs 0.68. Rival B (not held) is out, and E (not let in between two POOL instructions) too: the second sum got in behind the drive it met, in every step. But the narrower theory that was tested behind it, that only the short form is held, was wrong (sum_stt).
- **Silu of the gate at no price.** Off by 0.6 us per step in its favour, once the sums are moved: what was hidden under 10.6 us of waits is not hidden under 1.25.
- **The branch back.** The term with the wrong engine in it: ACT's stall was priced at 0.8 us twice, and DVE's own, rival C, was given 0.06 because its loop is shorter (the trace counts 196 instructions of DVE in a turn and 411 of ACT). DVE stalls 2.66 us; less what the wait at unit 3 gives back, the two branches cost 2.8 us, 1.2 more than counted, where rival C had 6.5 more. ACT's stall of 3.55 us lies under it.
- **The convolution.** Right that PE has no room: 0.56 of 2.58 us kept. Rival D is out: the eight matmuls take 3.58 us a step where 3.45 were counted. The late fill of unit 19 (1.55 us) lay under PE's lateness, as said, and came out in best4 when PE was relieved.
- **PE's clock.** Missing from the sum. DVE's waits of 0.15 to 1.23 us at units 8 and 16 stood in the trace of before, and I took them as given. They are PE at the lower clock behind idle stretches of 2.3 to 3.1 us. The changed kernel's clock falls less often, but its waits are longer, and warm takes them away. Why a fall costs more here is open.
- **The query stretch.** Rival A is out: held 4.2 us twice (4.6 predicted), and the new buffers gave back 3.2, where the prediction had 1.0 for them (1.75 of gain, less a late context load of 0.7). Its 5.1 for the key projection cannot be added up from the terms that it writes, so that hitting 5.4 is luck in part. It writes 3.85 more from turn 1 to turn 2 and 1 less from turn 2 to turn 3, the transposes of blocks 1, 2 and 3 on PE, and measured are 4.4 more and 0.75 less. It does not write how late turn 1 comes (3.6, the first hold) and what the end of the stretch gives back (1.8).

## What to carry to other kernels

When work moves between two engines that hold each other up, count the phase at which it arrives there, not only its length: the same sum cost 0.68 or 2.44 us for a place one instruction apart, and an addition queued 0.07 us ahead of another engine's instruction cost that engine 4.2 us. When a wait is removed, list what it covered (here a branch stall and a silu), since each of them comes out at its own price. A wait put down to an engine that had long been done is the waiting engine's own, or a third one's.

## What the runs showed of the hardware

- A TENSOR_SCALAR of 1024 columns on DVE took 2.44 us where it met a running POOL instruction, 0.97 where little of that was left and 0.68 where POOL stood idle.
- A SCALAR_TENSOR_TENSOR of 1024 columns with both inputs in SBUF was held in the same way: 2.98 us, ending 1.1 us after POOL's instruction, and 1.22 where it started first. A multiply with one input in PSUM was not: 1.22 us, started 0.11 us behind a drive of POOL.
- POOL is held as well: its addition took 2.80 us instead of 2.35 beside DVE's short sum and 3.34 beside the long one, and its drive 3.03 where the long sum had started first.
- Behind a branch back DVE stood 2.66 and 2.68 us over a loop body of 196 counted instructions, ACT 3.55 and 3.71 us over 411. Written out, DVE runs on without a stall.
- In the steps the granted clock fell to its lower level (1.2 GHz) where PE had been idle for 1.9 to 3.1 us between short pieces of work, for about 1.7 us of lost clock each time, at other places in each kernel. Matmuls of zeros in these stretches kept it at the upper level (2.4 GHz) from the first step's unit 4 to the last unit.
